# Four products of constants per slot on TensorE while the merged stage fills

## What is computed

```python
h = layernorm(x + multihead(x, x, x, sa_wq, sa_wk, sa_wv, sa_wo, causal=True), ln1_g, ln1_b)
h = layernorm(h + multihead(h, encoding, encoding, ca_wq, ca_wk, ca_wv, ca_wo, causal=False), ln2_g, ln2_b)
ff = jax.nn.relu(h @ ff_w1.T + ff_b1) @ ff_w2.T + ff_b2
return layernorm(h + ff, ln3_g, ln3_b)
...
x = x * jax.nn.sigmoid(gate)
return x + q0
```

## Time and profile before

| | us |
|---|---|
| median of three executions | 1029.33 (1028.06 to 1033.78) |
| the profiled execution, its own time | 1023.21 |
| span of that execution, first to last instruction | 1021.5 |
| TensorE busy in the span | 835.2 (82%) |
| mean granted clock, as a share of full | 0.895 |

### The profile page before, as it was taken

How to read it: one execution, slowest core, us unless ns; L and a number is a source line. 1 busy time by engine, 2 the same in 40 slices (tenths; PEclk the granted TensorE clock), 3 DMA queues, 4 the chain that set the end, 5 groups by cost and what they waited for, 6 DMA issues and landing times. The chain is left out here.

```text
span 1021.5 us, 19656 instructions
## 1 busy us (share of the span) xinstructions
PE 835.2 (82%) x7264; PEld 684.1 (67%) x7264; DVE 634.9 (62%) x1315; ACT 481.3 (47%) x953; POOL 465.0 (46%) x584
## 2 busy tenths in 40 slices
PE   5965689999999988215778999999988888949997
PEld 4654567777777755214455777878877778949996
DVE  2533466767767766344568777888766566525664
ACT  4411145455555546122556666666554555334542
POOL 3003347666566647111224555555544455643440
PEclk9986799999999999655667999999999999967988
DMA  7393888877877750116434322222321000022433
GB/s 230 136 347 83 196 172 176 166 143 166 163 160 150 144 104 3 60 44 150 101 78 100 89 63 64 65 64 64 69 66 41 1 2 1 2 84 71 124 110 100
DMA packets 71103, 105.99 MB, mean 104 GB/s; under 512 B 21656, under 2 KB 60698, under 8 KB 66142
## 3 DMA queue, kind: packets, MB, share of 16 engines
q1 hardware_dynamic: 67244, 98.46, 41.0%
q10 hardware_dynamic: 3764, 6.29, 1.7%
HBM read 68.57 MB, written 35.62 MB: 102 GB/s over the span
## 5 line engine op out<-in xcount | busy, mean ns | idle before, releaser
L1283 DVE TENSOR_REDUCE a_nm<-a_s 128x2 f32<-128x512 f32 (+1 forms) x192 | 129.2, 681 | 83.3 <-PE a_s L1107 81.4
L1249 ACT ACTIVATE a_pT<-a_st 128x512 f32<-128x512 f32 x192 | 111.7, 594 | 108.5 <-PE a_st L1130 107.1
L976 POOL TENSOR_TENSOR c_hl<-c_hid,c_hh 128x256 fp32r<-128x256 f32 x128 | 95.1, 743 | 146.2 <-DVE c_hid L866 145.5
L697 ACT ACTIVATE c_pT<-c_st 77x512 f32<-77x512 f32 x128 | 75.6, 591 | 141.1 <-PE c_st L570 131.8
L616 PE MATMUL c_down<-fw,c_hh 128*128 128x256 f32 x512 | 116.0, 295 | 0.0
L866 DVE TENSOR_SCALAR c_hid<-c_up,ff_b_col 128x256 f32<-128x256 f32 x128 | 61.5, 480 | 74.6 <-ACT c_hh L721 74.5
L76 PE MATMUL c_up<-c_fxh,fw 128*128 128x256 f32 x512 | 102.0, 292 | 2.4 <-DVE c_hid L866 2.4
L1392 POOL TENSOR_SCALAR_AFFINE_SELECT a_pT<-a_pT 128x256 f32<-128x256 f32 (+1 forms) x192 | 89.2, 482 | 27.7 <-ACT a_pT L1249 27.3
L616 PEld LDWEIGHTS c_down<-fw,c_hh 128*128 128x128 f32 x512 | 87.7, 192 | 14.4 <-issue 14.4
L1130 PE MATMUL a_st<-a_sq,a_sk 98*128 98x256 bf16 (+1 forms) x512 | 74.7, 249 | 16.6 <-DMA a_sq<-a_mT 12.0
L76 PEld LDWEIGHTS c_up<-c_fxh,fw 128*128 128x128 f32 x512 | 80.2, 193 | 3.9 <-DVE c_hid L866 3.4
(11 more groups left out here) (242 smaller groups left out, 2294.6 us busy)
## 6 DMA issues: line engine op xcount, KB each, us to landing
qk_parts<-a_parts SPq DMA_DIRECT2D x16, 768.0 KB
a_sq<-qk_parts SPq DMA_DIRECT2D x16, 384.0 KB, 5.3
a_sk<-qk_parts SPq DMA_DIRECT2D x16, 384.0 KB, 7.1
q_parts<-c_parts SPq DMA_DIRECT2D x16, 384.0 KB, 5.4
c_sq<-q_parts SPq DMA_DIRECT2D x16, 384.0 KB
g_vv<-vv_rows SPq DMA_DIRECT2D x16, 308.0 KB
vv_rows<-x_vv SPq DMA_DIRECT2D x9, 512.0 KB, 2.9
x<-in_xT SPq DMA_DIRECT2D x16, 256.0 KB, 9.3
```

Of the source, the lines that this page charges most:

```text
L697: nc.scalar.activation(pT[g % NPT][:], st_ps[0:SC, :], ACT.Exp).then_inc(s_exp, 1)
L976: nc.gpsimd.tensor_tensor(hl[:, m, :], hid[n % NHID][:], f32(hh[:, m, :]), ALU.subtract).then_inc(s_hl, 1)
L1249: nc.scalar.activation(pT[g % NPT][:], st_ps[g % 2][:], ACT.Exp).then_inc(s_exp, 1)
L1283: nc.vector.tensor_reduce(nm[c % 2][:, QT * heads[0] + qt:QT * heads[-1] + qt + 1:QT], s_ps[g % 2][:].rearrange("p (h k) -> p h k", h=len( ...
```

## The change

A function `keep_clock(n)` is added, which issues n products of 128 partitions by 512 columns, with wo's first block as weights and w1's first block as what is streamed, both constants. They go into bank `up[0]`, which nothing reads before `up_tile(0)` writes it at g = 44. In each slot with g below 44 two stand ahead of `scores` and two behind it; the condition holds for the 32 slots with negative g too, 76 slots in all, so 304 products. They carry no wait and no increment of their own. No other engine's list changes.

```diff
             pe.wait_ge(made, 2 + NSTK)
+            def keep_clock(n):
+                for _ in range(n):
+                    mt(up[0][:], wo[0][:, 0, 0:P], w1[0][:, 0, 0:512], start=True, stop=True, skip_group_check=True)
+
             for n, s in slots:
                 g = U * n + s
+                if g < UP_LAG:
+                    keep_clock(2)
                 scores(n, s)
+                if g < UP_LAG:
+                    keep_clock(2)
                 scores_turned(g - ST_LAG)
                 if s == 0:
                     project_q(n + 2)
```

## The result

The changed kernel takes 1046.64 us in the median of four executions (1043.5 to 1050.94), the kernel before 1028.87 (four, 1028.06 to 1033.78). The ratio is 1.0165, 95% interval 1.0115 to 1.0216: **slower by 17.8 us** between the medians, where +12.6 was forecast. The profiled execution spans 1043.4 us against 1021.5.

What follows compares the result with a forecast made beforehand. Time to slot 44 was taken to count, bound by the opening's chain and a ring of key release and loads in the fill. Opening +11.8 and fill +0.8 gave +12.6 on 1029.33 us, 1042, range 1035 to 1048.

Steps and rivals of the forecast that it cites:

- rival 2: Fill: waits for DVE's maxima (9.9 us) come on top of the products; +20 us in all, 1049; chance 0.11.
- The four terms of the fill: Batch 0's scores to slot 44: +1.1, -0.3, +0.6 and -0.5 us, given as together about +0.8.
- The opening: Last memset to batch 0's scores: 52 products ahead of the first transposes, 130 ahead of the scores; +11.8 us.
- The price of a product: One fp32r product of 512 columns: 0.233 us at full clock, 0.43 us at half clock, weight load hidden.
- Rival 1: Products sharing weights are lighter, 0.215 us each; +9.4 us in all, 1039; chance 0.14.
- The ring: Third to fifth periods: 5.6 us from scores to key release plus 12.2 us of loads; stays the bound, +0.2 each.
- TensorE's side of it ... = 5.8 us against 5.6: Third to fifth periods: TensorE's work from slot 8c's scores to the key release grows only from 5.6 to 5.8 us.
- the waits are covered: Fill: products at 0.93 us per slot cover TensorE's waits, with real work at full clock.
- still fit in the 12.2 of the loads: Third to fifth periods: TensorE's work in the remaining slots, 10 to 11 us, fits within the 12.2 us of loads.
- First batches and last piece: Fill outside the ring: first period +1.1 us, second -0.3, last piece to slot 44 -0.5.
- Rival 3: Not slower: with loads within 10.5 us, periods shrink to TensorE's work at full clock; +2.8 us, 1032; chance 0.07.
- After 557 ... TensorE is the bound: Behind slot 44: clock nearly always full, TensorE the bound, nothing of the change there; delay carried to the end.

Runs made afterwards that it cites:

- open_only: The changed kernel with its products only in the 32 slots with negative g (128 of 304); 1.0108 of the time of the kernel before.
- four_ahead: The changed kernel with all four products of a slot ahead of the scores, none behind; 1.0182 of the time of the kernel before.
- ring_part: The kernel before plus 40 products, g 16 to 43, only from slot 8c's scores to slot 8c + 2's turned scores; ratio 1.0105.
- pauses_all: The kernel before plus products only where TensorE paused: 33 in the opening, two per slot at g 0 to 15, 80 from g 16; ratio 0.9966.
- before_no_ln: The kernel before with Exp in place of Ln in `deviation`, which takes the table loads away; ratio 0.9718.
- fill_only: The changed kernel with its products only in the 44 slots with g from 0 to 43 (176 of 304); 1.0130 of the time of the kernel before.
- half_width: The changed kernel with all 304 products at 256 instead of 512 columns; 1.0104 of the time of the kernel before.

## Why the prediction was right, and where not

The sign, the place and the range held (1035 to 1048, measured 1046.64), the range by 1.4 us and because it took in the near half of rival 2. The size was 5 us short. In the pieces the opening came out 1.2 us below the forecast and the fill 6.4 above it, so part of the miss in the fill is hidden in the total. (The four terms of the fill add up to +0.9, not +0.8.)

- **The opening**: forecast +11.8 (lower bound +9.4), measured +10.6, +11.5 and +11.2 in the change, open_only and four_ahead. First transposes forecast 14.5 us behind the memset, measured 13.3, 14.7 and 13.5. The price of a product was nearly right: 0.233, measured 0.227 inside a row at full clock and 0.236 over a block of 16 with its ends. What varies is the part at half clock, taken as 12 products: it was 6 in the change, 13 in open_only and 7 in four_ahead, at 0.43 us each. Rival 1, lighter products at 0.215 us, is out. The price of the Trainium skill, "TensorE: Matmul & The Clock Gate", section "Wait — 56ns, not 53.3ns?", 0.216, is not met by this type either.
- **The ring**: right in its form, and ring_part shows that its stretch is paid in full. The step that failed is "TensorE's side of it ... = 5.8 us against 5.6", and with it "the waits are covered". Measured were 6.2, 6.2 and 8.1. Some 0.4 us of it are pairs between bf16 groups at up to 0.55 instead of 0.47; the 2 us of batch 4 are ACT and DVE work of slots 30 and 31, for which the sum had no term. I counted what fits into TensorE's pause on TensorE, and not what the other engines did in it. That the rest "still fit in the 12.2 of the loads" was true of TensorE (pauses of 1.5, 0.3 and 0.6 us are left) and not of ACT.
- **First batches and last piece**: forecast +1.1, -0.3 and -0.5, measured +1.5, +0.6 and +1.4; the same omission, in the last piece at batch 5's keys (7.4 us against 6.3).
- **Rival 2**, that waits for ACT and DVE come on top, is the one that the fill's part of the result is nearest to: +7.2, where it gave about +8 and the forecast +0.8. Its ground was right in one place only. Over the fill TensorE's waits for the maxima fell from 9.9 us to 0.9 (those of its weight loads from 15.5 to 4.7), so they don't come on top as a whole. In batch 4's stretch they do: the weight loads wait 0.94 us for ACT's exponential and 0.75 and 0.56 for maxima there, 2.25 together, and the stretch is 1.9 us longer than batch 3's.
- **Rival 3** asked for loads of 10.5 us. In the ring of the change they stayed at 11.4 to 12.3. But the gain that it looked for exists by another way: full clock is worth 2.0 us per batch in the ring (3.6 against 5.6 us in batches 2 and 3 of pauses_all), if no product stands in its stretch and no table load hangs over into it.
- "After 557 ... TensorE is the bound" was wrong, though it cost the prediction nothing: before_no_ln is 27 us shorter there with TensorE's work unchanged.

## What to carry to other kernels

Work that keeps an engine warm must stand where that engine waits anyway; in an engine that works in order, put ahead of ready work it costs its full time, and inside the stretch that releases the next transfer it costs its time once per round. Before filling an engine's pause, list what the other engines do in that pause: here ACT loaded two tables and DVE took a root while TensorE paused, and where the pause was filled or came early they ran over into the next round. A pause that is left open can bring the clock down for the stretch behind it all the same (0.78 behind 2.12 us in fill_only). Compare such kernels by pieces that start at the same instruction, since stages ahead of the edit moved by up to 10 us here between executions.

## What the runs showed that I had not expected

The kernel's two table loads per batch (L711 and L713, 16 times 1.28 us each) are worth more than anything above: with one activation function in place of another the median falls from 1028.63 to 998.01 us, ratio 0.9718 (0.9678 to 0.9758). In the steady part a batch takes 21.8 us instead of 23.25 (batches 7 to 13), 1.4 less of the 2.57 that the two loads take on ACT, although TensorE is busy 95% of that time. From 600 to 740 us, six batches, TensorE waits for this before:

```profile
PE c_qm L76 <- DVE c_mT L824: 5.2, 6, 0.9
PE c_av L583 <- DVE c_tr L832: 1.4, 6, 0.2
```

c_mT hangs on ACT. Without the table loads the wait for it is gone, once a batch 0.9 us, and of the other 0.4 us are left. That is some 1 us of the 1.4 per batch. Another 11 of the 27 us come after the first scores of the last batch (from there to the last `down_tile` 118.9 us before, 107.9 without the loads). How the loads act there was not followed up. In these kernels the deviation is another number, so they show what the loads cost and are no replacement. A square root that needs no other table than Exp's would be the next change to try.

The clock could be low exactly where it counts and high on average: half_width had 0.85 over the fill and 0.65 from the scores of batch 4 to the keys. And a pause of about the same length ended either way: batch 3's scores came at full clock behind 1.52 us in the change and at a clock that fell to 0.50 (0.76 over the stretch) behind 1.43 us in four_ahead.
